# A fused transformer layer on one core: the stream's projection weights rounded by GpSimd instead of ScalarE

## The reference

```
x = x + attention_a(layernorm(x))     # 32 heads of 16, rotary, causal
x = x + ffn(layernorm(x))             # dense 512x512 + top-2 routed LoRA experts
x = x + attention_b(layernorm(x))     # grouped-query: 32 query heads of 128, 8 key/value heads
x = x + ffn(layernorm(x))
```

```
q, k, v = x @ Wq.T, x @ Wk.T, x @ Wv.T        # 4096, 1024 and 1024 columns
q, k = rmsnorm(q, q_norm_w), rmsnorm(k, k_norm_w)
scores = einsum(q, k) / sqrt(128)  + alibi bias, causal mask
out = softmax(scores) @ v
return out @ Wo.T                              # 4096 -> 512
```

## Time and profile before

| quantity | value |
|---|---|
| median of 3 runs | 1619.59 us (1617.97 to 1619.84) |
| the profiled execution, own time | 1617.08 us |
| its span in the trace | 1615.3 us |
| PE busy | 1511.1 us, 94% |
| DVE busy | 1115.7 us, 69% |
| ACT busy | 816.0 us, 51% |
| POOL busy | 417.9 us, 26% |
| granted TensorE clock, mean | 0.988 |

### The profile page before, as it was taken

The page is one execution under the profiler, slowest core; times in us unless marked ns, Lnnn a source line. Parts: engine busy times, 40 slices in busy tenths (PEclk is TensorE's granted clock), DMA queues, the critical chain, the costliest instruction groups (busy, mean ns, idle before and its releaser), DMA issues.

```text
span 1615.3 us, 25452 instructions
## 1 busy us (share of the span) xinstructions
PE 1511.1 (94%) x8968; PEld 1172.3 (73%) x8968; DVE 1115.7 (69%) x2866; ACT 816.0 (51%) x2115; POOL 417.9 (26%) x407
## 2 busy tenths in 40 slices
PE   3998999998897899999999999999999999999997
PEld 2863444443786788888888888888888888888776
DVE  5668777770665677677677677677767767767873
ACT  3523555566333455555555555556555555555531
POOL 4102000010543131331322223143133132224333
PEclk9997999999998999999999999999999999999999
DMA  4363443301200010100100000011010010001000
GB/s 149 97 139 54 54 59 49 41 2 56 64 8 24 17 27 1 40 27 1 40 8 19 14 28 27 1 40 27 1 40 27 1 40 7 20 6 35 1 20 33
DMA packets 40207, 54.28 MB, mean 34 GB/s; under 512 B 5776, under 2 KB 21392, under 8 KB 40080
## 3 DMA queue, kind: packets, MB, share of 16 engines
q1 hardware_dynamic: 40080, 52.65, 13.7%
HBM read 44.04 MB, written 8.39 MB: 32 GB/s over the span
## 4 chain that ended last, share of the span: by engine, by line
PE 59%; DVE 5%; issue 5%; ACT 4%; POOL 2%; ACTq 0%; DVEq 0%; POOLq 0%
PE ps L50 17%; PE ps L52 17%; PE ps L51 16%; PE ps L1520 6%; PE ps L1495 2%; DVE ab_qt_l L1772 1%; ACT ab_w_h L1626 1%; ACT ab_squares L1657 1%; DVE ab_pt_l L1780 1%; ACT prob L1645 1%; POOL ab_o_l L1416 1%; PE ps L241 1%; ACT ab_pt_h L1673 0%; PE ps L1497 0%; ACT ab_kt_h L1666 0%
## 5 line engine op out<-in xcount | busy, mean ns | idle before, releaser
L1645 ACT ACTIVATE prob<-prob,ab_neg_max 128x128 f32<-128x128 f32 (+7 forms) x256 | 201.1, 786 | 250.3 <-DVE ab_neg_max L1763 249.2
L1780 DVE TENSOR_TENSOR ab_pt_l<-ps,ab_pt_h 128x512 fp32r<-128x512 f32 x288 | 198.1, 688 | 79.4 <-ACT ab_pt_h L1673 78.5
L1673 ACT CAST ab_pt_h<-ps 128x512 fp32r<-128x512 f32 x288 | 172.1, 598 | 122.3 <-PE ps L1520 121.8
L1763 DVE CUSTOM_DVE_ANT_0 prob<-ps,rel 128x512 f32<-128x512 f32 (+3 forms) x256 | 146.0, 570 | 102.4 <-PE ps L52 101.5
L50 PE MATMUL ps<-ab_w_h,ab_xt_h 128*128 128x512 f32 (+1 forms) x512 | 186.3, 364 | 6.8 <-DVE ab_v_l L1800 6.6
L1041 DVE TENSOR_REDUCE ra_part_max<-ps 128x1 f32<-128x512 f32 (+3 forms) x318 | 156.5, 552 | 47.8 <-PE ps L943 28.7
L1520 PE MATMUL ps<-ident,prob 128*128 128x128 f32 x1152 | 173.4, 273 | 4.6 <-DVE ab_qt_l L1772 3.3
L1788 DVE TENSOR_SCALAR prob<-prob,ab_recip 128x128 f32<-128x128 f32 (+7 forms) x256 | 169.3, 661 | 9.1
L52 PE MATMUL ps<-ab_w_h,ab_xt_l 128*128 128x512 f32 (+1 forms) x512 | 174.1, 340 | 0.0
L51 PE MATMUL ps<-ab_w_l,ab_xt_h 128*128 128x512 f32 (+1 forms) x512 | 173.5, 339 | 0.0
L1405 POOL TENSOR_TENSOR ab_rms<-ab_ms_eps,neg_half 128x5 f32<-128x5 f32 x64 | 76.2, 1191 | 311.5 <-DVE ab_ms_eps L1805 310.6
(11 more groups left out here) (231 smaller groups left out, 3482.6 us busy)
## 6 DMA issues: line engine op xcount, KB each, us to landing
f_raw<-in_wqkv SPq DMA_DIRECT2D x32, 384.0 KB, 3.7
f_raw<-in_wbo SPq DMA_DIRECT2D x32, 256.0 KB, 2.6
ra_first_rows<-parts SPq DMA_DIRECT2D x36, 128.0 KB, 7.1
parts<-pa_stage SPq DMA_DIRECT2D x12, 256.0 KB, 2.9
parts<-f_raw SPq DMA_DIRECT2D x12, 256.0 KB, 3.4
ra_q_st<-parts SPq DMA_DIRECT2D x24, 128.0 KB, 6.0
ra_k_st<-parts SPq DMA_DIRECT2D x24, 128.0 KB, 6.6
f_raw<-in_wf SPq DMA_DIRECT2D x8, 324.0 KB, 3.3
```

The source lines that it names most:

```text
L1645: act.activation(prob[:, t % 2, h, 0:w], prob[:, t % 2, h, 0:w], ACT.Exp, bias=neg_max[:, t % 2, h, pieces_per_head(t % NT) - 1:pieces_per ...
L1673: act.copy(pt_h[:, n % PT, :], ring_bank("p", u, j)).then_inc(pt_high, 1)
L1763: dve.tensor_tensor_reduce(out=prob[:, t % 2, h, k0:k1], in0=ps[:, n % 2, a:b], in1=const["rel"][:, SLIDE - i * P + k0:SLIDE - i * P + k1] ...
L1780: dve.tensor_tensor(pt_l[:, n % PT, :], ring_bank("p", u, j), pt_h[:, n % PT, :].bitcast(F32), ALU.subtract).then_inc(emptied, 1)
```

## The change

The cast of the next group's projection weights moves from ScalarE's queue to GpSimd's, in front of the subtraction of the same piece. GpSimd now waits for the raw piece and for `projected` itself. The four pairs are in slots 2, 3, 6 and 7 of GpSimd's step i = 5, where the subtractions alone were in slots 3 to 6. Within one slot GpSimd's order is output split, root, weights.

```diff
+            def split_both(n, read):
+
+                columns, high, low = raw_of(n)
+                pool.wait_ge(raw_in[n % KC], 16 * (n // KC + 1))
+                pool.wait_ge(projected, read)
+                pool.tensor_copy(high, raw[:, n % KC, 0:columns]).then_inc(split_high, 1)
+                split_low(n)
+
...
-                    if i == 5 and 3 <= s < 3 + KC and g + 1 < KVB and t >= 0:
-                        split_low(2 * KC * (g + 1) + s - 3)
+                    if i == 5 and s in (2, 3, 6, 7) and g + 1 < KVB and t >= 0:
+                        split_both(2 * KC * (g + 1) + (2, 3, 6, 7).index(s), KC * (t + 2) + (2, 3, 6, 7).index(s) + 1)
...
-                    if i == 5 and 2 <= s < 2 + KC and g + 1 < KVB and t >= 0:
-                        act.wait_ge(projected, KC * (t + 2) + s - 1)
-                        split_high_of(2 * KC * (g + 1) + s - 2)
```

## The result

The changed kernel took 1604.23 us in the median of 4 runs (1603.27 to 1604.81), the kernel before 1618.78 us beside it: a ratio of 0.991 with a 95% interval of 0.9893 to 0.9927, 14.6 us less. The forecast was 1603.7 us, 15.9 us less than the 1619.59 us it started from.

A forecast was written before the change was run, and what follows sets the result against it. TensorE, busy 94% of the span, was taken as the bound, losing 2.27 us in each of seven exchange steps: 1617.08 - 15.9 = 1601.2 us profiled, plus 2.5 for the median, 1603.7 us; range 1600.5 to 1612.5.

The forecast's parts named there:

- seven exchange steps: Stream steps in which weights are exchanged, step 13 among them; each to become 2.27 us shorter, 15.9 us in all.
- first `normalise`: VectorE's 128x768 operation at 708.82 in step 13; to fall into GpSimd's second subtraction, about 1.2 us instead of 1.93.
- second `normalise`: VectorE's next one in step 13; to fall at 712.9 into GpSimd's idle time, 0.6 us instead of 1.02.
- third `normalise`: VectorE in step 13; to fall at 716.4 into GpSimd's third cast, taking about 0.9 us instead of 1.31.
- output split ends: GpSimd's split behind the first two pairs; to end at 711.9 instead of 712.6, wanted by TensorE only in slot 7.
- fourth `normalise`: VectorE early in the next step; to meet the last subtraction, ending 0.8 us later than shifted, needed 1.5 us after.
- four late starts: TensorE starts later than their kind's spacing in step 13; 1.96 us, 2.27 us with slower first matmuls, all recoverable.
- the three on the path: ScalarE's weight casts in front of the `ab_pt_h` TensorE waits for; pushing it by 0.72 + 0.73 + 0.72 = 2.17 us.
- coupling with VectorE: VectorE's `normalise` waits for the GpSimd instruction under way, not its queue; 0.62 us idle, 1.93, 1.02, 1.31 in step 13.
- partly filled gap: Rival, 20%: third `normalise` also waits for the subtraction, 1.0 to 1.1 us stays in each step; gain 8 us, 1611.6 us.
- slower rival: Rival, 9%: VectorE gets its turn only when GpSimd's queue is drained; each step ends 1.6 us later, 1631 us.
- no-change rival: Rival, 9%: gaps return in the next step, or VectorE was not waiting for ScalarE; 1617 to 1622 us.

The follow-up runs named there:

- first series: The changed kernel's first comparison against the kernel before, median 1604.23 us; the same kernel compared again in five rounds gave 1602.83 us, ratio 0.9901.
- cast_twice: Changed kernel with each of GpSimd's four casts done twice at the same places: 1602.44 us, ratio 0.9898 to the kernel before.
- no_cast_halves: Changed kernel with GpSimd casting one column of 768 and each subtraction made in two halves of 384 columns: 1603.06 us, ratio 0.9905 to the kernel before.
- first_only: Against the kernel before, only piece 0 of each exchange is cast by GpSimd; ScalarE casts pieces 1 to 3: 1610.28 us, ratio 0.9941.
- no_cast: Changed kernel with GpSimd casting one column of 768 instead of the whole piece, subtractions whole: 1608.41 us, ratio 0.9931 to the kernel before.
- all_ahead: Changed kernel with all four pairs in GpSimd's slot 3, in front of output split and root: 1614.1 us, ratio 0.9967 to the kernel before.
- halves: Changed kernel with whole casts and each subtraction made in two instructions of 384 columns: 1603.48 us, ratio 0.99 to the kernel before.

## Why the prediction was right

The mechanism and the number both came out. Point by point for step 13, the after times less the 0.27 us of offset:

| step of the prediction | forecast | measured |
|---|---|---|
| seven exchange steps, each | -2.27 us | -2.29 us |
| GpSimd's 128x768 cast | 0.9 us | 0.82 to 0.83 us |
| first pair starts | 704.1 | 704.2 |
| first `normalise` | 1.2 us | 1.23 us |
| second `normalise` | 0.6 us | 0.62 us |
| third `normalise` | about 0.9 us | 0.96 us |
| `ab_pt_l` of block 3 | 713.95 | 713.96 |
| output split ends | 711.9 | 711.9 |
| root ends | 716.0 | 716.0 |
| end of `scale_qk` | 718.4 | 718.2 |
| `project` of the next step starts | 719.31 | 719.31 |
| median | 1603.7 us | 1604.23 and 1602.83 us |

Not all of this is equally earned. The 1.23 us of the first `normalise` holds for step 13 alone; in the other six it took 1.00 to 1.03. The split's "709.6 and (0.61 + 1.3)" adds up to 711.5, not 711.9; 711.85 comes out with the 0.94 us of a cast behind a `normalise`. The fourth `normalise` was to end 0.8 us later than in a plain shift and ended 0.5 later. And the median came within 0.5 us of the forecast in the first series by luck in part: the base was 0.8 us lower than the one reckoned with (1618.78 against 1619.59) and the gain 1.3 us smaller. The chances at the end (within 10%, slower 8%) also do not quite fit the 9% given to each of the two rivals.

**The bound.** TensorE's four late starts, 2.27 us with their slower first matmuls, were all that the step was said to give, and all of it came. That GpSimd no longer bounds the step is shown from both sides: 3.6 us more in its queue (cast_twice) change nothing, and neither does leaving out nearly all of the casts, once the subtractions are halved (no_cast_halves).

**ScalarE's casts.** The value of 2.17 us for the three on the path was their push on `ab_pt_h`, and alone they bring 1.87 us of TensorE's time; the prediction did not say what they would bring alone. The first one was indeed free on ScalarE's side: the `ab_pt_h` behind it starts at 708.73 (709.00 less the offset) without it and at 708.72 with it. But moving it brings 1.31 us through GpSimd; the prediction had the earlier end of the first `normalise` (710.05 instead of 710.75), and gave it no price of its own.

**The coupling with VectorE.** "`normalise` waits for the GpSimd instruction under way, not for its queue" is what first_only, no_cast and the halved subtractions show with durations between 0.62 and 2.25 us: in every kernel a held-up `normalise` of an exchange ends 0.40 to 0.43 us behind the GpSimd instruction in which it asked. "Then runs alone" is not quite it, since alone it takes 0.62 us; one that asked 0.12 us before the end of a cast (710.00 in no_cast) took no longer than that. The rule of the Trainium skill, GPSIMD Engine Reference, section 8 (Key points), that GpSimd contends with VectorE instructions in a two-port mode or with two SBUF inputs, agrees with the traces: both `normalise` (one SBUF tensor; its mode no trace shows) and, in all_ahead, `ab_ms_eps` (two inputs) are held up. The prediction took from it that four more GpSimd instructions would mean more collisions. They didn't cost more: in step 13 the four `normalise` lost 0.61 + 0 + 0.34 + 1.05 = 2.0 us to GpSimd, and 1.31 + 0.40 + 0.69 + 0 = 2.4 us before. The 0.40 there comes from the one subtraction of the step that the earlier trace rows leaves out:

```profile
713.02 1.83 POOL L1392 TENSOR_TENSOR ab_w_l<-f_raw,ab_w_h 128x768 fp32r<-128x768 f32 x1 [0.42 <-ACT ab_w_h L1626]
```

**The rivals.** The partly filled gap (1611.6 us) did not come true here, but it is real: no_cast has something like it, with 0.85 us of the 2.29 us left in a step against the 1.0 to 1.1 reckoned. The prediction named the third `normalise` for it. In no_cast the third alone did not do it, but there it ended 12.27 us behind `turn_qk` (719.15 less 706.88), and in the rival 13.48 (719.18 less 705.70), so the rival's own price stays untested. That the tenths of a us between ends decide was said; that less work could lose them was not. The slower rival (VectorE gets its turn only when the queue is drained) is excluded by the changed kernel, whose first `normalise` ended 0.42 us behind a subtraction with a cast, and the output split, right behind it, and by all_ahead, where the same holds in a queue without a pause. The no-change rival is excluded by the equal other steps: the fourth `normalise` did take 1.67 us in step 13, and the next step kept its 19.41 us.

**The shortfall.** The first series gained 14.6 us against the 15.9 forecast, the second 16.1. No term of the sum was off by that: the seven steps gave 16.0 us in both traces. What differed lies in front of the stream, where the granted clock was lower, and in the last store; the forecast had about 2 us of scatter in its range. Why the clock was lower there stays open.

## What to carry to other kernels

Look first for what the busiest engine starts late, in one period of a regular kernel, and add it up: that is the most that any change there can give, and here it was the gain to 0.02 us a step. When work goes to GpSimd, ask not how much but which GpSimd instruction is under way when VectorE wants to run an operation that the traces show being held up: a replay of the few instructions on the three engines told the first three `normalise` of step 13 to 0.1 us. Where such a request falls just behind the start of a long instruction, cutting that instruction in two is worth a try: it took the loss away in no_cast_halves, while in halves it made the longest wait shorter and another one longer, at no change in time.

## What the runs showed of the hardware

- Less work on GpSimd made the kernel 5.6 us slower (no_cast), because in six of seven exchanges two requests of VectorE then fell 0.01 us behind the starts of long instructions. One of them was lost by 0.01 us in one exchange (839.35 against 839.36) and won by 0.2 us in another (710.20 against 710.00), 1.69 against 0.62 us.
- A five-element operation with two SBUF inputs on VectorE took 0.81 instead of 0.15 us beside a GpSimd subtraction, and ended 0.04 us behind it; a held-up `normalise` ends 0.40 to 0.43 us behind.
- The waiting goes both ways: GpSimd's 128x512 cast took 0.95 instead of 0.61 us and its subtraction 2.03 instead of 1.84 us behind a `normalise`.
- GpSimd's cast from SBUF to SBUF took 0.61 us for 512 columns and 0.83 for 768, less than in proportion; its two-input subtraction took 1.3 and 1.84 us. ScalarE's cast of the same 768 columns took 0.86 us, but the next instruction in its queue starts 0.72 us after it, and on GpSimd 0.90 us (704.47 to 705.37), so in its queue a cast costs GpSimd more.
